# Reordering the first group of a gated cross-attention and expert kernel

## What is computed

```python
def proj(x, W, b):
    return (x @ W.T + b).reshape(x.shape[0], x.shape[1], H, Dh).transpose(0, 2, 1, 3)
q = apply_rope(proj(query, Wq, bq)); k = apply_rope(proj(key, Wk, bk)); v = proj(value, Wv, bv)
q = q * Dh ** (-0.5)
scores = jnp.where(mask4, neg, jnp.einsum('bhqd,bhkd->bhqk', q, k))
probs = jax.nn.softmax(scores, axis=-1)
out = jnp.einsum('bhqk,bhkd->bhqd', probs, v)
...
x = x + jnp.tanh(g_xattn[0]) * xattn(_layernorm(x), ctx, ctx, ...)   # out @ Wo.T + bo
x = x + jnp.tanh(g_ffn[0]) * ffn(_layernorm(x), ...)                 # top 2 of 32 experts, 16 adapters
```

## Time and profile before

| | |
|---|---|
| median of three runs | 797.49 us (796.78 to 798.66) |
| profiled execution | 796.95 us |
| its span, first to last instruction | 795.2 us |
| TensorE busy | 667.8 us, 84% |
| VectorE busy | 505.3 us, 64% |
| ScalarE busy | 407.6 us, 51% |
| GpSimd busy | 323.0 us, 41% |
| mean granted TensorE clock | 0.926 of full |
| first scores start | 28.62 us |

### The profile page before, as it was taken

One profiled execution on the slowest core, in us unless ns is written; L12 is line 12 of the kernel. 1 busy time (PEld: TensorE's weight loads), 2 busy tenths in 40 slices (PEclk: granted clock), 3 DMA queues, 4 the chain that ended last, 5 costly groups with the idle time before them and its releaser, 6 DMA issues.

```text
span 795.2 us, 17502 instructions
## 1 busy us (share of the span) xinstructions
PE 667.8 (84%) x5190; PEld 525.0 (66%) x5190; DVE 505.3 (64%) x1384; ACT 407.6 (51%) x1598; POOL 323.0 (41%) x339
## 2 busy tenths in 40 slices
PE   6799999999999999999885111089999999999993
PEld 3456665656666566667553000079999999999992
DVE  5665785766867677785897898934444444444441
ACT  1467777876877878787763563012222222222230
POOL 3343362443525534351111000036565656666542
PEclk8999999999999999999997555589999999999997
DMA  5600020200202002010102401028898889898931
GB/s 165 241 1 24 25 56 17 70 26 24 69 1 70 25 24 70 0 47 2 47 17 74 138 1 23 0 67 260 249 283 242 268 244 275 244 278 230 274 64 14
DMA packets 57422, 84.44 MB, mean 106 GB/s; under 512 B 11282, under 2 KB 28304, under 8 KB 57360
## 3 DMA queue, kind: packets, MB, share of 16 engines
q1 hardware_dynamic: 47168, 73.04, 28.0%
q0 software_dynamic: 9216, 9.76, 7.8%
q10 hardware_dynamic: 976, 0.96, 0.4%
HBM read 71.04 MB, written 12.69 MB: 105 GB/s over the span
## 4 chain that ended last, share of the span: by engine, by line
PE 55%; ACT 18%; DVE 17%; issue 5%; DMA 1%; ACTq 1%; POOL 1%; DVEq 0%; POOLq 0%
PE pair L824 19%; PE bank L834 10%; ACT arena L1104 8%; PE pair L1411 5%; DVE arena L1272 5%; PE bank L1376 3%; DVE arena L682 3%; PE pair L1420 3%; PE bank L1439 2%; PE pair L1406 2%; ACT arena L486 2%; PE bank L844 2%; ACT arena L1056 2%; ACT arena L1092 2%; PE bank L1355 1%
## 5 line engine op out<-in xcount | busy, mean ns | idle before, releaser
L1104 ACT ACTIVATE arena<-pair,arena 112x112 f32<-112x112 f32 x512 | 176.0, 366 | 61.0 <-DVE arena L1272 57.2
L824 PE MATMUL pair<-arena,we 128*128 128x140 f32 x1024 | 138.2, 283 | 0.8 <-ACT arena L744 0.6
L788 DVE SCALAR_TENSOR_TENSOR arena<-arena,pair 128x140 f32<-128x140 f32 x160 | 47.6, 298 | 137.0 <-ACT arena L752 137.0
L729 POOL DMA_INDIRECT rows_out<-arena,slot_row x64 | 94.4, 1476 | 90.5 <-DVE arena L776 74.8
L824 PEld LDWEIGHTS pair<-arena,we 128*128 128x128 f32 x1024 | 128.4, 190 | 1.9 <-issue 1.9
L752 ACT ACTIVATE arena<-pair 128x140 f32<-128x140 f32 x160 | 46.0, 288 | 147.3 <-PE pair L824 147.3
L1104 ACT ACTIVATION_READ_ACCUMULATOR arena<-pair,arena 112x1 f32 x512 | 110.1, 215 | 0.0
L718 POOL DMA_INDIRECT arena<-rows,slot_row x64 | 62.6, 978 | 113.6 <-issue 113.6
L834 PE MATMUL bank<-arena,we 128*128 128x140 f32 x512 | 83.3, 286 | 0.0
L1272 DVE TENSOR_REDUCE arena<-pair 112x8 f32<-112x896 f32 x64 | 69.3, 1082 | 20.2 <-PE pair L1411 19.2
L1420 PEld LDWEIGHTS pair<-tab,arena 112*112 112x112 f32 x512 | 51.9, 134 | 31.2 <-issue 29.5
(11 more groups left out here) (193 smaller groups left out, 1180.0 us busy)
## 6 DMA issues: line engine op xcount, KB each, us to landing
we<-w_experts_in SPq DMA_DIRECT2D x192, 256.0 KB, 4.3
wa<-w_adapters_in SPq DMA_DIRECT2D x16, 384.0 KB, 5.7
arena<-ctx_in SPq DMA_DIRECT2D x8, 448.0 KB, 4.4
arena<-x_in SPq DMA_DIRECT2D x8, 448.0 KB, 3.6
rows_out<-arena SPq DMA_DIRECT2D x8, 448.0 KB, 3.3
rows<-arena SPq DMA_DIRECT2D x8, 448.0 KB, 3.4
arena<-rows,slot_row POOLq DMA_INDIRECT x64, 4.4
rows_out<-arena,slot_row POOLq DMA_INDIRECT x64
```

The costliest lines, as they stand in the source:

```text
L729: nc.gpsimd.indirect_dma_start(d["out"], bass.IndirectOffsetOnAxis(ap=slot_row[:, h, e:e + 1], axis=0), yr[e % 2][:, h, :], None, compute_ ...
L788: signal(dve, nc.vector.scalar_tensor_tensor(gs[m % 2], th[m % 2], 1.0, banks[m % 4][:, 0:CAP], ALU.add, ALU.mult), s_gs, n + 1)
L824: last = nc.tensor.matmul(banks[m % 4][:, part * CAP:(part + 1) * CAP], w[:, col0:col0 + 128], xet[j % 2][:, c, :], start=(c == 0), stop=( ...
L1104: last = nc.scalar.activation(pr[s % 2][:, j, :], banks[BS[s % 4]][0:T, j * T:(j + 1) * T], ACT.Exp, bias=nmx[s // 2 % 2][:, s % 2, j:j + ...
```

## The change

The first group is prepared in another order. V 0 moves from step 9 to step 2, between keys and transposes. The normalisation moves from step 2 to step 0, ahead of both key rotations, and these move to steps 0 and 1. VectorE's statistics move ahead of the two scalings and the casts, and the scaling of the output bias from the start to step 8. The queries' rotation is split: batch 0 in steps 6 and 7, the other three batches in the steps 0 and 1 of the next call, behind the first reduction. The first scores wait for a new semaphore, `first_queries_roped`; the wait for `roped` moves to the scores of batch 1. The value weights get a semaphore of their own. The items of the first group get fixed banks, X 0 and X 1 two of the score banks. The unread products are now 3 behind X 1 and 14 behind V 1, where they were 12 behind K 1 and 1 behind X 1.

```diff
--- before.py
+++ after.py
@@ -144,9 +144,10 @@
 
 FRONT = [(0, "K", 0), (2, "K", 1), (3, "V", 0), (4, "X", 0), (5, "X", 1), (6, "Q", 0), (8, "Q", 1), (11, "V", 1)]
 
-FRONT_FIRST = [(0, "K", 0), (2, "K", 1), (4, "X", 0), (5, "X", 1), (6, "Q", 0), (7, "Q", 1), (9, "V", 0), (10, "V", 1)]
-ROTATE_FIRST = (1, 4, 7, 8)
-WARM_FIRST = {("K", 1): 12, ("X", 1): 1}
+FRONT_FIRST = [(0, "K", 0), (1, "K", 1), (2, "V", 0), (4, "X", 0), (5, "X", 1), (6, "Q", 0), (7, "Q", 1), (9, "V", 1)]
+ROTATE_FIRST = (0, 1, 6, 7)
+WARM_FIRST = {("X", 1): 3, ("V", 1): 14}
+LN1_FIRST, BIAS_FIRST = 0, 8
 OUT = [(NU * b + 9, "O", b) for b in range(GB)]
 ROUTE = [(GU + 10, "T", 0), (GU + 11, "T", 1), (GU + 14, "S", 0), (GU + 15, "H", 0)]
 HIDDEN = ROUTE[-1][0] - GU
@@ -205,6 +206,8 @@
 
 
 BS, BO, BM = (0, 1, 2, 3), 4, (5, 6, 7)
+BANKS_FIRST = {("K", 0): BM[0], ("K", 1): BM[1], ("V", 0): BM[2], ("X", 0): BS[2], ("X", 1): BS[3],
+               ("Q", 0): BM[0], ("Q", 1): BM[1], ("V", 1): BO}
 
 
 def head_of(k, j):
@@ -355,7 +358,8 @@
     fill = hpre[0:HC, 0:2 * ROW].rearrange("p (s c) -> p s c", s=2)
     zero = hpre[0:HC, 0:2 * C].rearrange("p (s c) -> p s c", s=2)
 
-    s_tab, s_const = sem("tables_in"), sem("weights_in")
+    s_tab, s_const, s_wv = sem("tables_in"), sem("weights_in"), sem("value_weights_in")
+    s_q0 = sem("first_queries_roped")
     s_wk, s_wq, s_bqk, s_bo = sem("key_weights_in"), sem("query_weights_in"), sem("qk_bias_in"), sem("out_bias_in")
     s_filled, s_gl = sem("filling_made"), sem("gates_in")
     s_fo = sem("filling_out")
@@ -881,7 +885,8 @@
         nc.sync.dma_start(ctxt[0], d["ctx"][0]).then_inc(s_ctx[0], 16)
         nc.sync.dma_start(xin, x_rows[:, 0:GB, :]).then_inc(s_xin, 16)
         nc.sync.dma_start(wq, d["wq"]).then_inc(s_wq, 16)
-        for dst, name in ((wv, "wv"), (wo, "wo"), (r1t, "r1t"), (r1s, "r1s"), (r1b, "r1b"), (r2t[:], "r2t")):
+        nc.sync.dma_start(wv, d["wv"]).then_inc(s_wv, 16)
+        for dst, name in ((wo, "wo"), (r1t, "r1t"), (r1s, "r1s"), (r1b, "r1b"), (r2t[:], "r2t")):
             nc.sync.dma_start(dst, d[name]).then_inc(s_const, 16)
 
         def fill_slots():
@@ -1037,7 +1042,7 @@
         act.wait_ge(s_gate, 2)
 
         def item(q, par, kind, what, j, n, first, tail):
-            src = banks[BM[n % 3 if first else kind]]
+            src = banks[BANKS_FIRST[what, j] if first else BM[kind]]
             if what == "H" and tail:
                 src = banks[BS[HIDDEN_BANK]]
             wait(act, s_m[kind], len(KINDS[kind]) * q + n + 1)
@@ -1173,18 +1178,22 @@
                                     tab[:, TAB["cos"]].unsqueeze(1).to_broadcast([128, GB, T]),
                                     ALU.mult).then_inc(s_rot, 1)
 
-        def rotate_all(z):
-
-            wait(dve, s_proj, z + 1)
-            dve.wait_ge(s_rope, 2)
-            nc.vector.stream_shuffle(prot[z % 2], proj[z % 2],
+        def rotate_first(z, some):
+
+            n = some.stop - some.start
+            cols = slice(some.start * T, some.stop * T)
+            dve.wait_ge(s_proj, z + 1)
+            dve.wait_ge(s_rope, z - 1)
+            nc.vector.stream_shuffle(prot[z % 2][:, cols], proj[z % 2][:, cols],
                                      mask=[i + DH // 2 if i % DH < DH // 2 else i - DH // 2 for i in range(32)])
-            by_batch = lambda a: a.rearrange("p (b t) -> p b t", b=GB)
-            each = lambda name: tab[:, TAB[name]].unsqueeze(1).to_broadcast([128, GB, T])
+            by_batch = lambda a: a[:, cols].rearrange("p (b t) -> p b t", b=n)
+            each = lambda name: tab[:, TAB[name]].unsqueeze(1).to_broadcast([128, n, T])
             link(nc.vector.tensor_tensor(by_batch(pcos[z % 2]), by_batch(proj[z % 2]), each("cos"), ALU.mult))
-            dve.sem_inc(s_rot, 1)
+            if some.stop == GB:
+                dve.sem_inc(s_rot, 1)
             link(nc.vector.tensor_tensor(by_batch(prot[z % 2]), by_batch(prot[z % 2]), each("sin"), ALU.mult))
-            nc.vector.tensor_tensor(qt[0][:, z - 2, :], pcos[z % 2], prot[z % 2], ALU.add).then_inc(s_rope, 1)
+            last = nc.vector.tensor_tensor(qt[0][:, z - 2, cols], pcos[z % 2][:, cols], prot[z % 2][:, cols], ALU.add)
+            last.then_inc(s_rope if some.stop == GB else s_q0, 1)
 
         def values(q, par, j, kind, n, bank):
 
@@ -1280,7 +1289,9 @@
                 for lag in range(2):
                     for kind, back, what, j, n in at_step(s, EMPTIED[lag], front, own, prev):
                         if what == "V" and j == lag:
-                            values(g - back, (par + back) % 2, j, kind, n, banks[BM[0 if own else n % 3]])
+                            if not own and j == 0:
+                                dve.wait_ge(s_const, 16 * 7)
+                            values(g - back, (par + back) % 2, j, kind, n, banks[BM[0] if own else BANKS_FIRST[what, j]])
                 for kind, back, what, j, n in at_step(s, 1, front, own, prev):
                     if what == "O":
                         residual(g - back, (par + back) % 2, j, kind, n)
@@ -1292,7 +1303,7 @@
                     ln1_stats(g + 1)
                 if prev and s == LN2_APPLY:
                     ln2_apply(g - 1, 1 - par)
-                if front and s == (LN1_APPLY if prev or not own else LN1_SECOND[1]):
+                if front and s == (LN1_FIRST if not own else LN1_APPLY if prev else LN1_SECOND[1]):
                     ln1_apply(g + 1)
                 for part in XF_STATS.get(s, ()) if prev else ():
                     xf_stats(g - 1, part)
@@ -1302,7 +1313,13 @@
                     if own or z < 2:
                         rotate(g + 1, z)
                     else:
-                        rotate_all(z)
+                        rotate_first(z, slice(0, 1))
+                if front and not own and s == BIAS_FIRST:
+
+                    dve.wait_ge(s_bo, 16)
+                    nc.vector.tensor_scalar(gbo, gbo, gates[0:T, 0:1], None, ALU.mult).then_inc(s_gate, 1)
+                if own and not prev and s < 2:
+                    rotate_first(2 + s, slice(1, GB))
                 if own and not front:
                     if s == SHIFTED[0]:
 
@@ -1320,16 +1337,14 @@
                     if not own and s == STEPS - 1:
                         dve.sem_inc(s_scr, 1)
 
+        ln1_stats(0)
         dve.wait_ge(s_gate, 1)
         nc.vector.tensor_scalar(gates[:, 2:3], gates[:, 1:2], 0.5, None, ALU.mult).then_inc(s_setup, 1)
         dve.wait_ge(s_bqk, 16)
         nc.vector.tensor_scalar(bqk[:, 2:4], bqk[:, 2:4], DH ** -0.5, None, ALU.mult).then_inc(s_gate, 1)
-        ln1_stats(0)
         dve.wait_ge(s_tab, 16)
         nc.vector.tensor_copy(identb, tab[0:T, TAB["ident"]][:, 0:T]).then_inc(s_setup, 1)
         nc.vector.tensor_copy(causalb, tab[0:T, TAB["causal"]]).then_inc(s_setup, 1)
-        dve.wait_ge(s_bo, 16)
-        nc.vector.tensor_scalar(gbo, gbo, gates[0:T, 0:1], None, ALU.mult).then_inc(s_gate, 1)
         groups(nc.vector.Fori, group, link, DVE_LINKS)
         routing_vector(dve, link)
         experts_vector(dve, link)
@@ -1341,8 +1356,12 @@
                 nc.tensor.matmul(out[:, 0:NT], r1t[:, c, :], xft[:, c, :], start=(c == 0), stop=False)
 
         def item(q, par, loads, kind, what, j, n, first, tail, between):
-            out = banks[BM[n % 3 if first else kind]]
-            wait(pe, s_mf[kind], n - 2 if first else FIRST[kind] + len(KINDS[kind]) * q + n)
+            out = banks[BANKS_FIRST[what, j] if first else BM[kind]]
+            if not first:
+                wait(pe, s_mf[kind], FIRST[kind] + len(KINDS[kind]) * q + n)
+            elif what == "Q":
+
+                pe.wait_ge(s_proj, j + 1)
             if what in "XT":
 
                 rows = xn if what == "X" else xf
@@ -1392,12 +1411,14 @@
                 last = nc.tensor.matmul(out[:, 0:NT], r1s, stt, start=False, stop=True)
             last.then_inc(s_m[kind], 1)
 
-        def scores(g, par, s):
+        def scores(g, par, s, prev):
 
 
 
             b, k = s // NU, s % NU
-            if s == 0:
+            if s == 0 and not prev:
+                pe.wait_ge(s_q0, 2)
+            elif s == (0 if prev else NU):
                 wait(pe, s_rope, 4 * (g + 1))
             if k == 0:
                 wait(pe, s_kz, GB * g + b + 1)
@@ -1470,7 +1491,7 @@
         def group(g, par, front, own, prev, loads=1):
             for s in range(STEPS):
                 if own and s % 2 == 0:
-                    scores(g, par, s)
+                    scores(g, par, s, prev)
                 for back, u in unit_at(s, TURN, own, prev):
                     turn(g - back, u)
                 for back, u in unit_at(s, WEIGH, own, prev):
@@ -1483,10 +1504,12 @@
                         elif what == "Q":
                             pe.wait_ge(s_wq, 16)
                         else:
-                            pe.wait_ge(s_const, 16 * 8)
-                            pe.wait_ge(s_setup, 6)
+                            pe.wait_ge(s_wv, 16)
```

(3 more changed lines are left out.)

## The result

| | before | after |
|---|---|---|
| median | 798.04 us (796.78 to 799.89, 10 runs) | 795.42 us (794.50 to 799.18, 10 runs) |
| profiled execution, its span | 796.95, 795.2 | 794.79, 793.0 |
| mean granted TensorE clock | 0.926 | 0.927 |

The ratio of after to before is 0.9968 (95% interval 0.9956 to 0.9980): 2.6 us faster, where 3.3 was forecast. The median itself, 795.42, stands 1.2 above the forecast of 794.2, and half of that lies in the kernel before, which ran at 798.04 beside it and not at 797.49.

A forecast was written before the change was run, and what follows sets the result against it. The chain of waits preparing the first group of four batches bounds the start. Gain 5.6 to the first scores, less 2.1 for cut rotations and 0.2 behind: 3.3 us, median 794.2, range 792.2 to 797.8.

The forecast's parts named there:

- second block of rotations: Other three batches' second query tile, rotated on VectorE between first and second reduction: all 2.1 us on the path.
- lead there: Gain left at the second reduction, after the second block of rotations: 3.5 us.
- the fourteen: Unread products on TensorE behind the second value item, ahead of the first scores: 2.85 us added.
- Full clock: TensorE in the first group: the granted clock holds through idle stretches of 1.4 and 1.65 us.
- The first rival: The clock falls in the first group, back at 21.8: scores at 26.6, nothing gained, 797.5 us; 12 in 100.
- Small pieces against GpSimd: Batch 0's query rotation on VectorE: 0.2 us per undisturbed 112-column operation, else the rest of GpSimd's; ready at 22.1.
- The first block: Other three batches' first query tile, rotated on VectorE behind the first reduction: 2.1 to 2.3 us, hidden to 0.1.
- Behind that: After the second reduction: TensorE's clock falls before the next group's first values; 0.2 us lost.
- The assumption: Attention after the start: a shift that has passed through all in-order engines stays to the end.

The follow-up runs named there:

- whole: The changed kernel with the queries of all four batches rotated whole before the first scores: 0.9947 of the kernel before, median 794.34 us.
- fewer unread products: The changed kernel with 8 unread products behind the second value item instead of 14: 0.9968 of the kernel before, median 796.13 us.
- forty-eight on ScalarE: The changed kernel with 48 semaphore increments that nobody waits for on ScalarE, ahead of its first expert instruction: 0.9970 of the kernel before.
- forty-eight on VectorE: The changed kernel with 48 semaphore increments that nobody waits for on VectorE, ahead of its first expert instruction: 0.9975 of the kernel before.
- The late values: The changed kernel with the first value item behind the queries, 20 unread products behind the keys, none behind the values: 0.9968, median 796.08 us.

## Why the prediction was right

**The start.** Each piece stood where its step put it:

| step | forecast | after |
|---|---|---|
| GpSimd's first arithmetic | 10.3 | 10.29 |
| normalisation | 11.8, takes 1.4 | 11.71, takes 1.38 |
| transposes | 13.35 | 13.24 |
| first query item | 15.25 | 15.17 |
| end of second values | 20.15 | 20.14 |
| batch 0's queries ready | 22.1 | 21.86 |
| first scores | 23.0 | 22.63 |
| second block of rotations | 2.1 | 2.03 |
| second reduction | 31.2 | 30.93 |
| lead there | 3.5 | 3.75 |

The largest miss is at the first scores, 0.37. The second values end at 20.14 as forecast, and the unread products start before that in the rows, so the fourteen cost 2.5 on the path and not 2.85: a group's busy time overlaps the groups beside it and isn't the distance to the next.

One reading in the prediction's first paragraph was wrong, and no number hung on it: the transfer of the output bias did not hold VectorE for 8.58. VectorE had other work until 11.40 (in the timeline of the kernel before, the second cast starts at 11.19 and takes 0.21), and the scaling starts at 11.44 without a wait and takes 0.35.

**The clock in the first group.** Full clock was taken, since the idle stretches of 1.4 and 1.65 are shorter than the 2.10 that was followed by a fall. They were 1.24 and 1.48, and the clock held in both profiles of the changed kernel. But of six profiles of kernels that are the same up to the queries, two had a fall there (whole at 15.0, fewer unread products at 15.8). The first rival was more alive than its 12 in 100; its price was too high, since the fall lasted 3.4 and not 6.8 and cost 1.6 at the scores.

**Small pieces against GpSimd.** For 112 columns 0.2 undisturbed was taken, and the whole rest of GpSimd's operation otherwise. Measured 0.26 to 0.27, and for the first tile, beside GpSimd (VectorE, then GpSimd):

```profile
17.81 0.76 DVE L1191 TENSOR_TENSOR we<-arena,tab 128x112 f32<-128x112 f32 x1
18.60 1.20 DVE L1194 TENSOR_TENSOR arena<-arena,tab 128x112 f32<-128x112 f32 x1
19.84 1.04 DVE L1195 TENSOR_TENSOR arena<-we,arena 128x112 f32<-128x112 f32 x1
```

```profile
17.31 1.13 POOL L962 TENSOR_TENSOR arena<-arena,tab 128x448 f32<-128x448 f32 x1
18.52 1.15 POOL L971 TENSOR_TENSOR arena<-we,arena 128x448 f32<-128x448 f32 x1
19.81 0.93 POOL L978 TENSOR_TENSOR arena<-arena,tab 128x448 f32<-128x448 f32 x1
```

Each of VectorE's three ends within 0.15 behind one of GpSimd's: 18.57 behind 18.44, 19.80 behind 19.67, 20.88 behind 20.74. For 448 columns the end comes 0.48 behind GpSimd's (24.12 behind 23.64 in the earlier trace rows). They run one behind the other, as the exclusive lock of the Trainium skill's page "SBUF — State Buffer" (Who interferes with whom) has it; by a shared port I would expect no such ends.

**The two blocks.** The first block was taken as hidden and was: from 25.21 it lies where VectorE had idled 2.19. The second lies on the path with 2.03; with whole rotation the second reduction comes 4.38 behind the first and not 6.74, and that 2.4 is the price of the cut at this place. That run also shows what the working didn't ask: whether the cut gains more than it costs. It brings the scores 1.9 forward and the second reduction 0.4 back.

**Behind that: the term that was mis-sized.** 0.2 lost was taken, because the clock would fall and the next group's first values take between 1.8 and 3.6. They took 3.76, all of it at half clock, against 2.80, and the lead went from 3.75 to 3.45: 0.3 in this execution. But the term isn't one number. What was lost between the second and the eighth reduction, by kernels with the same code up to there: 0.28 (after), 0.31 (the same kernel again), 0.32 (forty-eight on ScalarE) and 5.0 (forty-eight on VectorE, half clock for 20.5 us). The late values lost 1.1, with 10.2 us of half clock. So the 0.2 was right for three of four executions and far off for the fourth.

**Carried to the end.** The assumption was that a shift which has gone through all engines stays. It held from the third to the 23rd reduction (3.45 to 3.53). That it was still 3.44 at the last was luck: VectorE's three pauses took 1.1, which the working had at nothing, and before's dearer fall of the clock gave 1.0 back. In the second profile of the changed kernel, whose own fall came later and cost as much as before's, 3.70 had become 2.58. The four profiles with the changed kernel's code throughout attention (after, again, forty-eight on ScalarE, on VectorE) lead at the last reduction by 3.44, 2.58, 3.72 and -1.29, 2.1 in the mean; the runs of the same four show 2.0 to 2.6. So the forecast of 3.3 and the 2.6 measured most likely part here, in these pauses and in falls of the clock that differ from execution to execution. How much is due to each, four profiles can't say. The profiled span shows 2.2 only, and that is the pause in expert 0, which before's first profile alone lacks.

**What the parts are worth.** Of the parts that had a run, the normalisation ahead of the rotations carries the most: 1.2 us by the trace, nearly the whole gain by the runs. The place of the bias scaling is worth 0.2 to 0.4 by one profile. Early values and the number of unread products can't be told from nothing. Cutting the rotations costs about 2. The earlier statistics had no run of their own; that they are worth the 1.0 by which GpSimd starts earlier (10.29 and 11.34) is argued from the rows, and so is what the full clock at the queries gives. Without the cut the kernel is 0.53% faster than before (0.9931 to 0.9963), and this is the version to keep.

## What to carry to other kernels

Where two engines get in each other's way, look first for an order in which the shared step meets nobody: here four instructions took 1.38 instead of 3.0, and that was the part whose loss the runs showed. Before cutting a step so that its first piece is early, find who pays for the rest: ask for the second wait behind the cut, not the first. Compare at a mark that both traces have (here every reduction), at all of them, since a lead that is the same at both ends can be a sum of losses and gains; and profile the kernel before twice before a difference of 1 us far from the change is put down to the change.

## What was new of the hardware

**Half clock under work.** The granted clock stayed at 0.50 for 20.5 us with TensorE busy for 17.90 of 19.00. The Trainium skill's page "TensorE: Matmul & The Clock Gate" (Part 1: The HAM clock gate) says that activity releases the throttle; this stretch doesn't agree with that alone, since the same code in after was back at 1.00 after 6.8 us. These products are small or float32, with dependences between them; which of that matters wasn't tried.

**The place of a fall differs from execution to execution.** With the same instructions up to there it began at 31.6, 32.2, 32.1 and 32.9, after 2.0 to 3.4 us without a product; in before at 38.9, a microsecond after the products had begun again, in both profiles. Each of the four has one more fall, of 3.4 us, near 168, 176, 264 and 173. Filling one gap moved the fall to the next, in the one profile of it.

**A pause of VectorE at one instruction of the loop**, 0.53 (once 0.51) where it is otherwise 0.17, in each of the three passes, in ten of ten profiles of kernels with the cut rotation and in none of four without. The loop's code is the same; what differs stands ahead of it. Its cause is open.

**A pause of some 3 us of ScalarE in expert 0**, in thirteen of fourteen profiles, of both kernels and wherever the instructions ahead stand. Its cause is open.
